# Attention scores of a split-fp32 kernel: two products a tile in place of three

## What is computed

```python
q = (x @ W_q).reshape(b, n, HEADS, DIM_HEAD)
k = (context @ W_k).reshape(b, j, HEADS, DIM_HEAD)
sim = jnp.einsum('bihd,bjhd->bhij', q, k) * scale
sim = jnp.where(mask[:, None, None, :], sim, max_neg)
attn = jax.nn.softmax(sim, axis=-1)
out = jnp.einsum('bhij,bjhd->bihd', attn, v).reshape(b, n, INNER)
...
x = x + _L0_xattn_ref(_layernorm(x, axis=-1), ctx_768, mask_BxS2_bk0, ...)
x = x + _L0_ffn_ref(_layernorm(x, axis=-1), L0_ffn_Wr, L0_ffn_W1, L0_ffn_W2)
```

## Time and profile before

| | us |
|---|---|
| median of 3 runs (2360.76 to 2361.67) | 2361.15 |
| profiled execution, its span | 2362.9 |
| PE busy in the span | 2108.3 (89%) |
| DVE busy | 1001.1 (42%) |
| ACT busy | 687.1 (29%) |
| POOL busy | 511.7 (22%) |
| the attention passes, from the first unit's scores to the last pass's end | about 50 to 720 |

### The profile page before, as it was taken

One profiled execution on the slowest core, in us unless ns is written; L12 is line 12 of the kernel. 1 busy time (PEld: TensorE's weight loads), 2 busy tenths in 40 slices (PEclk: granted clock), 3 DMA queues, 4 the chain that ended last, 5 costly groups with the idle time before them and its releaser, 6 DMA issues.

```text
span 2362.9 us, 32573 instructions
## 1 busy us (share of the span) xinstructions
PE 2108.3 (89%) x11976; PEld 1864.8 (79%) x11977; DVE 1001.1 (42%) x2199; ACT 687.1 (29%) x1672; POOL 511.7 (22%) x551
## 2 busy tenths in 40 slices
PE   4998999889992899899899979989997998998997
PEld 3877877787771789798789869878886887987896
DVE  5666665666666334233322433331233344324221
ACT  3543453463341213212211321221122133123110
POOL 2443453354344011111010101100110110110100
PEclk9999999999995899999999989999998999999999
DMA  4122022112103214213310321240133124123111
GB/s 143 39 77 77 16 60 76 40 36 76 47 14 125 98 27 120 77 26 80 104 35 6 105 79 40 45 121 32 27 80 104 40 69 115 39 45 104 40 14 14
DMA packets 95540, 148.57 MB, mean 63 GB/s; under 512 B 7920, under 2 KB 49312, under 8 KB 95376
## 3 DMA queue, kind: packets, MB, share of 16 engines
q1 hardware_dynamic: 79632, 109.36, 14.3%
q0 software_dynamic: 15744, 36.71, 8.8%
HBM read 110.66 MB, written 35.39 MB: 62 GB/s over the span
## 4 chain that ended last, share of the span: by engine, by line
PE 62%; issue 4%; DVE 1%; ACT 0%; DMA 0%; POOL 0%; POOLq 0%; DVEq 0%; ACTq 0%
PE psH L1412 31%; PE psY L1412 29%; PE psX L1425 1%; PE psI L1454 1%; DMA xg<-xn_rows,gid_next 0%; DVE onehot L1307 0%; ACT w_hi L939 0%; ACT xgT_hi L1260 0%; DVE xgT_lo L1290 0%; POOL out_dram L1231 0%; DVE moves L1299 0%; POOL xg L1222 0%; POOLq L1154 0%; DVE ys L1341 0%; DVE eq_t L1295 0%
## 5 line engine op out<-in xcount | busy, mean ns | idle before, releaser
L1348 DVE SCALAR_TENSOR_TENSOR hT_lo<-psH,hT_hi 128x384 fp32r<-128x384 f32 (+1 forms) x384 | 209.9, 547 | 939.1 <-ACT hT_hi L1266 939.0
L1412 PE MATMUL psH<-xgT_hi,w_hi 128*128 128x384 f32 (+2 forms) x1536 | 495.4, 323 | 92.2 <-issue 92.2
L1266 ACT ACTIVATE hT_hi<-psH 128x384 fp32r<-128x384 f32 (+1 forms) x384 | 185.4, 483 | 1108.5 <-PE psH L1412 1108.4
L1412 PE MATMUL psH<-xgT_lo,w_hi 128*128 128x384 f32 (+2 forms) x1536 | 490.5, 319 | 3.5 <-issue 3.5
L1412 PE MATMUL psH<-xgT_hi,w_lo 128*128 128x384 f32 (+2 forms) x1536 | 490.5, 319 | 1.6 <-issue 1.6
L1412 PEld LDWEIGHTS psH<-xgT_hi,w_hi 128*128 128x128 f32 x1536 | 300.9, 196 | 118.2 <-issue 103.1
L1412 PE MATMUL psY<-w_hi,hT_hi 128*128 128x512 f32 (+1 forms) x992 | 392.6, 396 | 0.0
L1412 PE MATMUL psY<-w_lo,hT_hi 128*128 128x512 f32 (+1 forms) x992 | 391.6, 395 | 0.0
L1412 PE MATMUL psY<-w_hi,hT_lo 128*128 128x512 f32 (+1 forms) x992 | 391.1, 394 | 0.0
L1412 PEld LDWEIGHTS psH<-xgT_lo,w_hi 128*128 128x128 f32 x1536 | 300.8, 196 | 18.0 <-issue 5.1
L1412 PEld LDWEIGHTS psH<-xgT_hi,w_lo 128*128 128x128 f32 x1536 | 300.3, 195 | 0.0
(11 more groups left out here) (192 smaller groups left out, 2962.8 us busy)
## 6 DMA issues: line engine op xcount, KB each, us to landing
stage<-in_L_ffn_W_dram SPq DMA_DIRECT2D x128, 512.0 KB, 4.2
x_sb<-in_x_dram SPq DMA_DIRECT2D x8, 896.0 KB, 8.2
x_res<-in_x_dram SPq DMA_DIRECT2D x8, 896.0 KB, 5.8
out_dram<-x_res SPq DMA_DIRECT2D x8, 896.0 KB, 4.8
xn_rows<-xn SPq DMA_DIRECT2D x8, 896.0 KB, 4.7
c_sb<-in_ctx_dram SPq DMA_DIRECT2D x16, 375.0 KB
out_dram<-zrow SPq DMA_DIRECT2D x9, 256.0 KB, 4.4
out_dram<-ys,sid_now POOLq DMA_INDIRECT x72, 5.2
```

Of the source, the lines that this page charges most:

```text
L1266: nc.scalar.activation(hT[0][:, f % 2, 0:cols(k)], psH[f % 2][:, 0:cols(k)], ACT.Relu).then_inc(h_hi, 1)
L1348: nc.vector.scalar_tensor_tensor(out=hT[1][:, f % 2, 0:n], in0=psH[f % 2][:, 0:n], scalar=0.0, in1=f32(hT[0][:, f % 2, 0:n]), op0=ALU.max, ...
L1412: mm = nc.tensor.matmul(out, stationary(a, c), moving(b, c), start=first and c == chunks[0] and j == 0, stop=last and c == chunks[-1] and ...
```

## The change

k is stored by head and not by part: `k0` holds head 0's high part in partitions 0 to 63 and its low part in 64 to 127, `k1` head 1's high part in 64 to 127 and its low part in 0 to 63. The high part of q is written into both halves of `q0_hi` and `q1_hi`; the low part stays in the head's own half, with zeros in the other. One matmul of q_hi with this k gives hi·hi + hi·lo, a second of q_lo with the same k gives lo·hi.

```diff
@@ -214,7 +214,8 @@
-        kT = [sb(f"k_{k}", [128, 2, TP * KC], F32R) for k in ("hi", "lo")]
+        kz = [sb(f"k{h}", [128, 2, TP * KC], F32R) for h in range(2)]
+        own = [slice(0, DH), slice(DH, 128)]
@@ -339,8 +340,7 @@
             for h in range(2):
-                for k in range(2):
-                    nc.gpsimd.memset(f32(qz[h][k][:]), 0.0).then_inc(zeros, 1)
+                nc.gpsimd.memset(f32(qz[h][1][:]), 0.0).then_inc(zeros, 1)
@@ -359,10 +359,15 @@
                 elif kind == "q":
-                    nc.scalar.activation(qz[0][0][0:64, i % 2, :], src[0:64, 0:TP * R], ACT.Copy)
-                    nc.scalar.activation(qz[1][0][64:128, i % 2, :], src[64:128, 0:TP * R], ACT.Copy).then_inc(proj_hi, 1)
+                    for h in range(2):
+                        nc.scalar.activation(qz[h][0][own[h], i % 2, :], src[own[h], 0:TP * R], ACT.Copy)
+                    for h in range(2):
+                        a = nc.scalar.activation(qz[h][0][own[1 - h], i % 2, :], src[own[h], 0:TP * R], ACT.Copy)
+                    a.then_inc(proj_hi, 1)
                 else:
-                    nc.scalar.activation(kT[0][:, i % 2, :], src[:, 0:TP * KC], ACT.Copy).then_inc(proj_hi, 1)
+                    for h in range(2):
+                        a = nc.scalar.activation(kz[h][own[h], i % 2, :], src[own[h], 0:TP * KC], ACT.Copy)
+                    a.then_inc(proj_hi, 1)
@@ -418,7 +423,9 @@
                 else:
-                    a, h, o = src[:, 0:TP * KC], kT[0][:, i % 2, :], kT[1][:, i % 2, :]
+
+                    nc.vector.tensor_tensor(kz[0][64:128, i % 2, :], src[0:64, 0:TP * KC], f32(kz[0][0:64, i % 2, :]), ALU.subtract)
+                    a, h, o = src[64:128, 0:TP * KC], kz[1][64:128, i % 2, :], kz[1][0:64, i % 2, :]
                 nc.vector.tensor_tensor(o, a, f32(h), ALU.subtract).then_inc(proj_done, 1)
@@ -619,9 +626,10 @@
-                            mm = product(psS[i % 2][0:R, it * NKEY:(it + 1) * NKEY],
-                                         lambda k, c: qz[h][k][:, hp % 2, at:at + R],
-                                         lambda k, c: kT[k][:, hp % 2, b * NKEY:(b + 1) * NKEY], 1)
+                            for k in range(2):
+                                mm = nc.tensor.matmul(psS[i % 2][0:R, it * NKEY:(it + 1) * NKEY], qz[h][k][:, hp % 2, at:at + R],
+                                                      kz[h][:, hp % 2, b * NKEY:(b + 1) * NKEY], start=k == 0, stop=k == 1,
+                                                      skip_group_check=True)
```

More of the change, by code:

```diff
@@ L396, in _ @@
                 if kind == "v" and i == 0:
-                    act.wait_ge(zeros, 6)
+                    act.wait_ge(zeros, 4)
                 split_hi(None, True, kind, i)
@@ L649, in _ @@
                 if kind == "v" and i == 0:
-                    pe.wait_ge(zeros, 6)
+                    pe.wait_ge(zeros, 4)
                 proj(None, True, kind, i, 1)
```

## The result

The changed kernel takes 2429.96 us (median of 4 runs, 2426.51 to 2436.74) against 2361.41 us: the ratio is 1.0286, with a 95% interval of 1.0267 to 1.0305. It is slower by 68.6 us. The forecast had the direction and most of its mechanism, but 2400 us and a range that ended at 2409.

A forecast was written before the change was run, and what follows sets the result against it. It took the end of DVE's split of k, not busy PE, to bound most stretches. 36.6 + 7.7 + 1.6 = 45.9, less 5.5, 1.3 and 0.3, gave +38.8 on 2361.15: 2400 us, range 2377 to 2409.

The forecast's parts named there:

- the 5.5 us of units 0 to 2: Units before q1 and after the tail: PE keeps 0.23 us in each, 0.69 a pass, 5.5 in all.
- The price of the splits: Added ACT copies and DVE subtractions, halves of k priced as whole instructions: 45.9 us before savings, 38.8 after.
- behind q3: Step q3 k3: the chain starts at the split of k, so 1.60 us later in each pass.
- from q1 to q2: Step q1 k1: the mask after k's split, PE's unit 4 and q2 come 1.60 us later in each pass.
- the tail: Before the router logits: two more ACT copies ahead of q0's subtraction cost 1.10 us in each of 7 passes.
- the transfer's hiding: Before q1 in three passes: 0.41 us of delay vanishes in PE's wait for `v_lo`, 1.3 us in all.
- The prologue's 1.6: Prologue: the added split work has no cover there and costs 1.60 us once.
- The step q2 k2: After q2 and k2: the later mask had waited for PE, so the delay is 1.37 us a pass, not 1.60.
- The held instructions: DVE's split: both k halves and the mask are held by partition changes, 2 x 0.68 us; otherwise 3.8 us less.
- third rival: By the reflection: PE at 1.2 GHz behind 31 waits, 46.5 us, chance 0.02; the prediction text given lacks it.
- Everything hidden: Whole kernel: added splits all hidden and the 29.9 us saving counts whole, giving 2331 us; chance 0.07.
- PE's saving in full beside the delays: Whole kernel: delays of 45.9 us are real but PE's 29.9 counts too, +16.0, 2377 us; chance 0.10.

The follow-up runs named there:

- e3_two_products: The kernel before with two score matmuls a tile, q_hi times k_lo left out and its splits untouched: 2363.74 us, ratio 0.9998.
- e1b_fill_ahead: The changed kernel with overwritten filler matmuls in PE's longest waits, those of the tail ahead of the router logits' wait: 2409.52 us, ratio 1.0200.
- e4_q_copies: The kernel before with two further ACT copies of q, to the other partition half, in all steps but the prologue's: 2395.66 us, ratio 1.0140.
- e5_k_halves: The kernel before with k's high copy and low part each made in two halves of 64 partitions, in place: 2401.01 us, ratio 1.0151.
- e2_third_back: The changed kernel with three score matmuls a tile again, the first product made twice: 2432.66 us, ratio 1.0279.

## Why the prediction was right or wrong

**What bounds the kernel: right.** PE, 91% busy in a pass, is not what sets its time; e3_two_products takes 29.9 us of matmuls away and gives 0.9998. One detail was off: the 5.5 us of units 0 to 2 are kept only where the transfer of x doesn't take them back.

**The price of the splits: right, a few us short.** The sum had 45.9 us before the savings and 38.8 after them; the end of attention in e1b_fill_ahead, where the clock holds, gives 44.4 after them, 5.6 more. By terms: behind q3 (229.0 - 215.7) / 8 = 1.66 for the 1.60 forecast; from q1 to q2 (97.4 - 83.3) / 8 = 1.76 for 1.60, as PE now comes to q1 before ACT is done with unit 2, and the first copy of q starts 2.88 us after q1's first matmul in place of 2.66; the tail (195.7 - 187.9) / 7 = 1.11 for 1.10; the saving of units 0 to 2 less the transfer's hiding 4.1 to 5.4 for the 4.2 forecast (5.5 - 1.3). The prologue's 1.6 did not come: the first unit started at 49.43, not later than 49.84.

**The step q2 k2: wrong in its reason.** The forecast gave it 1.37 because the mask of unit 7 had waited for PE. It measured (117.2 - 103.7) / 8 = 1.69, and 0.81 for 0.60 in e4_q_copies. In the changed kernel that mask did gain (it stands 1.2 behind the mask of unit 6, for 1.43), but what the chain goes through is ACT: exponential of unit 6, `pT_hi`, exponential of unit 7, `oT_hi`, all without a hole:

```profile
266.52 0.50 ACT L380 ACTIVATE probs<-probs,nmax 112x250 f32<-112x250 f32 x1 [1.75 <-DVE nmax L484]
...
267.51 0.52 ACT L386 ACTIVATE pT_hi<-psT 125x448 fp32r<-125x448 f32 x1
267.94 0.49 ACT L380 ACTIVATE probs<-probs,nmax 112x250 f32<-112x250 f32 x1
...
268.91 0.34 ACT L390 ACTIVATE oT_hi<-psO 128x224 fp32r<-128x224 f32 x1
```

The mask of unit 7 is ready before ACT comes to it (it starts at 266.94 on DVE, its last maximum is read by 267.70). That an instruction waited does not put it on the chain.

**The held instructions: right.** DVE's four subtractions stand 0.64, 0.65, 0.69 and 0.71 apart, each as long as it lasts, as the rule of the Trainium skill has it (VectorE: DVE Perf Modes, section on two Vector instructions with no wait between them); e5_k_halves shows the same, 0.68 and 0.71.

**The clock: the step that failed.** The sum priced everything at a granted clock of 1.00 and has no term for PE at 1.2 GHz. The prediction named that case as its third rival, with its place and a price of 46.5 us for 31 waits, and gave it 0.02, because all passes had run at 1.00 with waits such as 1.04. But the waits that the change makes are of another size, 2.33, 2.27 and 2.03 us. None of the rows says anything about such waits; the 3.29 us behind the passes of the kernel before, with a clock of 0.50 after it, was in the trace and was not read. The forecast had computed the 2.2 us itself and then did not use them. The fillers show what it cost: of the 70.3 us by which attention ends later, 25.9 are gone once PE is kept busy, 1.0286 against 1.0200 in the ratios. The rival's price was too high: its 3 us of slow clock behind each of 31 waits were an assumption, and the trace has a stretch behind some of the waits only, 3.5 to 6.9 us long, with half of the time lost in them off the path. It came on top of the likeliest case, not in its place; the range should have held the sum of both.

**The rivals.** Everything hidden (0.07) and PE's saving in full beside the delays (0.10) are refuted by e3_two_products and e2_third_back.

What stays open: why the same wait is followed by a slow stretch in one pass and not in the next (the tail takes 28.1 or 29.8 us in the same kernel, and e4_q_copies, with the same 2.03 us of waiting in the tail, slowed down there in two of seven only). Nor was the path behind attention followed, which varied by up to 12 us between kernels that do not differ there.

## What to carry to other kernels

An engine can be busy nine tenths of a loop and give nothing back when its work shrinks: ask which instruction releases it at the end of each stretch, and take the work away as a trial before paying for it elsewhere. An instruction over half of the partitions cost as much here as over all of them (0.67 and 0.68 us on DVE for 64x500, 0.68 for 128x500), so a layout that writes two halves separately doubles the work of the engines that copy. And where a change makes PE wait longer than it ever did, price the time behind the wait at half the clock as well: passes that ran at full clock with short waits don't rule it out, and a long wait elsewhere in the same trace may show it.

## What the runs showed of the hardware that was not expected

The clock did not go by the number of products alone: e2_third_back (three products) ran attention at about 0.94, little above the changed kernel (0.93), while e3_two_products, with two products and 53 us of waits before the products with v, spread in pieces of up to 1.5 us, ran it at 1.00. Attention of e1b_fill_ahead, its long waits filled, ran at 1.00 too, and so did e5_k_halves, with waits of 1.54 to 1.63 us in every pass, but for one stretch at the start.

Two waits of the changed kernel that are shorter than 2 us, before o3 and o5 of one pass,

```profile
267.08 0.37 PE L556 MATMUL psO<-pT_hi,v_hi 125*128 125x224 f32 x1 [1.80 <-DVE pT_lo L497]
...
272.10 0.37 PE L556 MATMUL psO<-pT_hi,v_hi 125*128 125x224 f32 x1 [1.46 <-DVE pT_lo L497]
```

were followed by matmuls at full speed in that pass: from 259.3 to 283.1 the granted clock is 0.99. That is not the rule for the first of them: in four of the eight passes a slow stretch began within 1.5 us behind it.

ACT's copies from PSUM to the other half of the partitions took the same 0.54 us for 64x448 as those that stay.
